# Graph network kernel, final update: node-row product made at the end of attention, means taken behind the message product, four node blocks per PSUM bank

## The reference, cut to what matters

```python
x = layernorm(x + attention_layer(x, edges))
h = relu(concat(x[src], x[dst]) @ Wm1 + bm1)
h = relu(h @ Wm2 + bm2)
messages = h @ Wm3 + bm3
agg = segment_sum(messages, dst) / clip(count, 1)
upd = relu(concat(x, agg) @ Wn1 + bn1) @ Wn2 + bn2
out = layernorm(x + (x + upd))
```

## Time and profile before

| | us |
|---|---|
| median of 3 runs | 1838.62 |
| lowest and highest | 1836.01, 1838.82 |
| the profiled execution, its own time | 1839.05 |
| its span in the trace | 1837.3 |
| PE busy | 1631.2 (89%) |
| DVE busy | 1577.7 (86%) |
| ACT busy | 1296.8 (71%) |
| POOL busy | 1176.0 (64%) |

### The profile page before, as it was taken

One profiled execution on the slowest core, in us unless ns is written; L12 is line 12 of the kernel. 1 busy time (PEld: TensorE's weight loads), 2 busy tenths in 40 slices (PEclk: granted clock), 3 DMA queues, 4 the chain that ended last, 5 costly groups with the idle time before them and its releaser, 6 DMA issues.

```text
span 1837.3 us, 52399 instructions
## 1 busy us (share of the span) xinstructions
PE 1631.2 (89%) x15380; PEld 1447.3 (79%) x15380; DVE 1577.7 (86%) x3374; ACT 1296.8 (71%) x2335; POOL 1176.0 (64%) x1197
## 2 busy tenths in 40 slices
PE   4778888777778777699999999999999999999986
PEld 3568777666667665499999999999999999999964
DVE  6999999778878767499999999999999999999976
ACT  5145777777777776577777777777777777777741
POOL 3135777767776612577777777777777777777710
PEclk9999999889898878799999999999999999999999
DMA  4135677788788734555555555555555555555511
GB/s 116 39 77 114 133 139 144 149 142 158 149 158 148 145 69 128 140 140 140 140 141 141 139 140 140 141 140 140 139 140 140 139 139 140 139 140 139 140 50 36
DMA packets 142000, 237.54 MB, mean 129 GB/s; under 512 B 27997, under 2 KB 92849, under 8 KB 141914
## 3 DMA queue, kind: packets, MB, share of 16 engines
q0 software_dynamic: 49632, 143.79, 32.4%
q1 hardware_dynamic: 89128, 91.13, 21.2%
q10 hardware_dynamic: 3154, 1.60, 0.4%
HBM read 186.67 MB, written 10.68 MB: 107 GB/s over the span
## 4 chain that ended last, share of the span: by engine, by line
PE 57%; DVE 1%; issue 0%; ACT 0%; DMA 0%; POOL 0%; POOLq 0%; DVEq 0%
PE ps L1300 12%; PE ps L1301 10%; PE ps L1306 10%; PE ps L1280 9%; PE psA L1318 6%; PE ps L1275 5%; PE ps L1285 2%; PE ps L1042 1%; PE ps L1053 1%; PE ps L1050 1%; PE psA L1061 0%; DVE x L1114 0%; DMA ga<-table_a,idx 0%; ACT u L1075 0%; POOL ga L1253 0%
## 5 line engine op out<-in xcount | busy, mean ns | idle before, releaser
L1253 POOL DMA_INDIRECT ga<-table_a,idx x784 | 766.8, 978 | 244.4 <-issue 82.6
L637 POOL DMA_INDIRECT head_n<-scr_eye,row_at x250 | 329.0, 1316 | 226.7 <-PE psC L683 106.2
L1300 PE MATMUL ps<-wm_hi,h_hi 128*128 128x256 f32 x1568 | 411.3, 295 | 0.7 <-ACT h_hi L1352 0.7
L1301 PE MATMUL ps<-wm_lo,h_hi 128*128 128x256 f32 x1568 | 390.8, 282 | 0.0
L1356 ACT ACTIVATE h<-ps 128x512 bf16<-128x512 f32 x392 | 234.1, 597 | 191.1 <-PE ps L1306 190.4
L1300 PEld LDWEIGHTS ps<-wm_hi,h_hi 128*128 128x128 f32 x1568 | 295.8, 189 | 31.8 <-ACT h_hi L1352 26.8
L1432 DVE TENSOR_TENSOR h<-rest,h 128x512 bf16<-128x512 f32 x392 | 269.4, 687 | 53.0 <-ACT h L1360 53.0
L1427 DVE SCALAR_TENSOR_TENSOR rest<-ps,h 128x512 f32<-128x512 f32 x392 | 268.6, 688 | 46.9 <-ACT h L1356 39.2
L1301 PEld LDWEIGHTS ps<-wm_lo,h_hi 128*128 128x128 f32 x1568 | 296.0, 189 | 0.0
L697 PE MATMUL psC<-ring_n,ring_m 128*126 x1320 | 229.2, 313 | 57.1 <-DVE ring_n L916 29.0
L1421 DVE SCALAR_TENSOR_TENSOR h_lo<-ps,h_hi 128x512 fp32r<-128x512 f32 x392 | 264.3, 692 | 3.1 <-ACT h_hi L1352 3.1
(11 more groups left out here) (192 smaller groups left out, 2529.0 us busy)
## 6 DMA issues: line engine op xcount, KB each, us to landing
dstb<-scr_dst SPq DMA_DIRECT2D x196, 126.0 KB
cnt<-stage SPq DMA_DIRECT2D x125, 195.3 KB
cnt<-stage SPq DMA_DIRECT2D x125, 109.9 KB
ga<-table_a,idx POOLq DMA_INDIRECT x784
bw<-table_b SPq DMA_DIRECT2D x196, 63.0 KB
table_b<-cnt SPq DMA_DIRECT2D x12, 336.0 KB
head_n<-scr_eye,row_at POOLq DMA_INDIRECT x250, 6.2
table_a<-pr SPq DMA_DIRECT2D x12, 224.0 KB
```

The lines of the kernel that those rows point to most:

```text
L637: pool.indirect_dma_start(head_n[:, w % HEADS, s, :], None, scr_eye, bass.IndirectOffsetOnAxis(ap=row_at[:, w % ROWS_AT, s:s + 1], axis=0) ...
L1253: pool.indirect_dma_start(ga[:, u, k, :], None, table_a, bass.IndirectOffsetOnAxis(ap=idx[:, u, k:k + 1], axis=0)).then_inc(gathered[u][k] ...
L1300: pe.matmul(ps2[q][:, t % 2, :], hi, w_hi[:, k, :], start=False, stop=True, skip_group_check=True)
L1301: pe.matmul(ps2[q][:, t % 2, :], hi, w_lo[:, k, :], start=False, stop=True, skip_group_check=True)
```

## The change

The product of `x1T` with `wa[0]` is taken out of Update and made at attention's end, into `T.xw` (2 x 3125 columns). `T.xw` is allocated for the whole program, and during attention serves as slots 0 and 1 of the probabilities; slots 2 and 3 are a tensor of their own, `upper`. So three of its products may be made once the last chunk of sums has been added (before the transposes of chunk 7), and eleven stand behind PE's last L741. They go through three PSUM banks; DVE copies ten of them out and ACT four.

In Update ACT writes each half of `T.xw` into the PSUM bank of `u1` ahead of the product with `msg`, which then accumulates on it. `T.agg` is no longer scaled; the scaling by `T.inv` is done on the product with `Wm3`, in the step that makes `msg`. The last product of a cut goes to one bank with four blocks side by side; ACT writes the bias `bb` there first, and DVE takes the cut in one instruction (`2 * x1 + bank`). Two small bf16 products with ones and a bias row open the two banks once. The load of `wn1` moves from SP's end of the sweep to attention's end, between `w` and `b1`, and PE waits for the three loads there (48 in place of 32).

The core of the diff:

```diff
+CUT_BLKS = 4
+NODE_CUTS = [(a * BLK, min(NBLK, a + CUT_BLKS) * BLK) for a in range(0, NBLK, CUT_BLKS)]
...
-        pr = sb("pr", [BLK, PR, N], fp32)
+        upper = sb("upper", [BLK, 2, N], fp32)
+        pr = [T.xw[0:BLK, 0, :], T.xw[0:BLK, 1, :], upper[:, 0, :], upper[:, 1, :]]
...
+        xw_banks = [psO[0], psO[1], psD]
+        XW = 2 * len(NODE_CUTS)
+        EARLY = 3
+        def xw_taken(n):
+            odd = [i for i in range(n + 1) if i >= XW // 2 and i % 2]
+            return (1, len(odd)) if n in odd else (0, n + 1 - len(odd))
...
             sp.dma_start(w.rearrange("p (c h) -> p c h", c=2), wm1.rearrange("(c f) h -> f c h", c=2)).then_inc(loaded, 16)
+            sp.dma_start(T.wa[:, :, :], wn1.rearrange("(c f) h -> f c h", c=2)).then_inc(loaded, 16)
...
-            pe.wait_ge(loaded, 32)
+            pe.wait_ge(loaded, 48)
+            def node_products(first, end):
+                for n in range(first, end):
+                    a, z = NODE_CUTS[n // 2]
+                    if n >= len(xw_banks):
+                        eng, count = xw_taken(n - len(xw_banks))
+                        pe.wait_ge(xw_read[eng], count)
+                    pe.matmul(xw_banks[n % len(xw_banks)][:, 0:z - a], T.wa[:, 0, (n % 2) * P:(n % 2 + 1) * P], T.x1T[:, a:z],
+                              start=True, stop=True).then_inc(xw_done, 1)
             for c in range(CH):
+                if c == CH - 2:
+                    pe.wait_ge(chunk_added, (2 * TURNS_A + 1) * CH + len(banks))
+                    pe.wait_ge(edges_read, DCUTS)
+                    node_products(0, EARLY)
...
+            node_products(EARLY, XW)
...
+            def copy_products(first, end):
+                for n in range(first, end):
+                    if xw_taken(n)[0] == 0:
+                        a, z = NODE_CUTS[n // 2]
+                        dve.wait_ge(xw_done, n + 1)
+                        dve.tensor_copy(T.xw[:, n % 2, a:z], xw_banks[n % len(xw_banks)][:, 0:z - a]).then_inc(xw_read[0], 1)
...
+                if c == CH - 1:
+                    copy_products(0, EARLY)
+            copy_products(EARLY, XW)
```

Update, PE:

```diff
+        for bank in self.banks:
+            pe.matmul(bank[:, :], T.ones_b[:, :], T.bias_b[:, :, :].rearrange("p t h -> p (t h)"), start=True, stop=True,
+                      skip_group_check=True).then_inc(self.u2_opened, 1)
...
-                pe.wait_ge(self.mean_ready, c + 1)
...
+                pe.wait_ge(self.msg_ready, c)
                 for m in range(2):
                     n = 2 * (c - 1) + m
-                    if n >= 4:
-                        pe.wait_ge(self.u1_ready, n - 3)
-                    pe.matmul(psU[n % 4][:, 0:z - a], T.wa[:, 0, m * P:(m + 1) * P], T.x1T[:, a:z], start=True, stop=False)
-                    if m == 0:
-                        pe.wait_ge(self.msg_ready, c)
-                    pe.matmul(psU[n % 4][:, 0:z - a], T.wa[:, 1, m * P:(m + 1) * P], msg[:, (c - 1) % 2, 0:z - a], start=False, stop=True).then_inc(self.u1_done, 1)
+                    pe.wait_ge(self.u1_seeded, n + 1)
+                    pe.matmul(psU[n % 4][:, 0:z - a], T.wa[:, 1, m * P:(m + 1) * P], msg[:, (c - 1) % 2, 0:z - a],
+                              start=False, stop=True, skip_group_check=True).then_inc(self.u1_done, 1)
...
-                for i, b in enumerate(range(a // BLK, z // BLK)):
-                    if b >= 2:
-                        pe.wait_ge(self.u2_read, b - 1)
+                pe.wait_ge(self.u2_seeded, c - 1)
+                for i in range((z - a) // BLK):
                     for k in range(2):
-                        last = pe.matmul(psV[b % 2][0:BLK, 0:D], u1[:, c % 2, k, i * BLK:(i + 1) * BLK], T.wb[:, k, :], start=(k == 0), stop=(k == 1))
-                    last.then_inc(self.u2_done, 1)
+                        last = pe.matmul(psV[c % 2][:, i, :], u1[:, c % 2, k, i * BLK:(i + 1) * BLK], T.wb[:, k, :],
+                                         start=False, stop=True, skip_group_check=True)
+                last.then_inc(self.u2_done, 1)
```

Update, ACT and DVE:

```diff
+        def seed_u1(c):
+            a, z = cuts[c]
+            for m in range(2):
+                act.activation(psU[(2 * c + m) % 4][:, 0:z - a], T.xw[:, m, a:z], ACT.Copy).then_inc(self.u1_seeded, 1)
+        for c in range(2):
+            seed_u1(c)
...
+                if c >= 2:
+                    act.wait_ge(self.u2_read, c - 1)
+                else:
+                    act.wait_ge(self.u2_opened, c + 1)
+                blks = (z - a) // BLK
+                act.activation(psV[c % 2][:, 0:blks, :], T.bb[0:BLK, :].rearrange("p (o f) -> p o f", o=1).broadcast_to([BLK, blks, D]),
+                               ACT.Copy).then_inc(self.u2_seeded, 1)
+                if c + 2 < CUTS:
+                    act.wait_ge(self.u1_ready, 2 * c + 2)
+                    seed_u1(c + 2)
...
-                for k in range(2):
-                    last = dve.tensor_tensor(T.agg[:, k, a:z], T.agg[:, k, a:z], T.inv[:, a:z], ALU.mult)
-                last.then_inc(self.mean_ready, 1)
...
-                dve.scalar_tensor_tensor(T.x1[:, bs, :], T.x1[:, bs, :], 2.0,
-                                         T.bb[0:BLK, :].rearrange("p (o f) -> p o f", o=1).broadcast_to([BLK, z // BLK - a // BLK, D]),
-                                         ALU.mult, ALU.add).then_inc(self.doubled, 1)
...
-                dve.scalar_tensor_tensor(self.msg[:, (c - 1) % 2, 0:z - a], self.has[:, (c - 1) % 2, 0:z - a], T.b3[:, 0:1], psM[(c - 1) % 2][:, 0:z - a],
-                                         ALU.mult, ALU.add).then_inc(self.msg_ready, 1)
+                step(dve.tensor_tensor(at, psM[(c - 1) % 2][:, 0:z - a], T.inv[:, a:z], ALU.mult))
+                dve.wait_ge(self.has_ready, c)
+                dve.scalar_tensor_tensor(at, self.has[:, (c - 1) % 2, 0:z - a], T.b3[:, 0:1], at, ALU.mult, ALU.add).then_inc(self.msg_ready, 1)
...
-                for b in range(a // BLK, z // BLK):
-                    dve.wait_ge(self.u2_done, b + 1)
-                    dve.tensor_tensor(T.x1[:, b, :], T.x1[:, b, :], psV[b % 2][0:BLK, 0:D], ALU.add).then_inc(self.u2_read, 1)
+                dve.scalar_tensor_tensor(T.x1[:, bs, :], T.x1[:, bs, :], 2.0, psV[(c - 3) % 2][:, 0:(z - a) // BLK, :], ALU.mult, ALU.add).then_inc(self.u2_read, 1)
```

More of the change, by code:

```diff
@@ L403, in _, with attention @@
             act.activation(T.hx[:, :, D:D + 1], onesf[0:BLK, 0:NBLK + 1].rearrange("p (b o) -> p b o", o=1), ACT.Copy)
-def attention(nc, T, scr_eye, wm1, bm1, table_a, table_b):
+def attention(nc, T, scr_eye, wm1, bm1, wn1, table_a, table_b):
     with ExitStack() as ctx:
@@ L668, in sum_chunk @@
                     for k in range(2):
-                        last = pe.matmul(bank[0:BLK, a * W2:(a + 1) * W2], pr[:, (first + k) % PR, b * BLK:(b + 1) * BLK],
+                        last = pe.matmul(bank[0:BLK, a * W2:(a + 1) * W2], pr[(first + k) % PR][:, b * BLK:(b + 1) * BLK],
                                          hx[:, bass.ds(t * BPT + first + k, 1), 0:W2].rearrange("p o w -> p (o w)"), start=(k == 0), stop=(k == 1))
@@ L849, in _ @@
                     act.activation(b_st[:, s, 0:i, 1, :], rest[:, s, 0:i, :], ACT.Copy).then_inc(part_ready[1], 1)
+            for n in range(XW):
+                if xw_taken(n)[0] == 1:
+                    a, z = NODE_CUTS[n // 2]
+                    act.wait_ge(xw_done, n + 1)
+                    act.activation(T.xw[:, n % 2, a:z], xw_banks[n % len(xw_banks)][:, 0:z - a], ACT.Copy).then_inc(xw_read[1], 1)
         @block.vector
@@ L999, in __init__ @@
         self.T, self.out = T, out
-        self.cuts = [(a * BLK, min(NBLK, a + self.CB) * BLK) for a in range(0, NBLK, self.CB)]
-        CW = self.CB * BLK
+        self.cuts = NODE_CUTS
+        CW = CUT_BLKS * BLK
         self.has = sb("has", [P, 2, CW], fp32)
@@ L1006, in __init__ @@
         self.psM = [bank[:, :, :].rearrange("p t h -> p (t h)") for bank in ps2]
-        self.psV = psA
-        self.mean_ready = sem("mean_ready")
+        self.banks = psA
+        self.u2_opened = sem("u2_opened")
+        self.psV = [bank[0:BLK, :].rearrange("p (b f) -> p b f", f=D) for bank in psA]
+        self.u1_seeded = sem("u1_seeded")
+        self.u2_seeded = sem("u2_seeded")
         self.has_ready = sem("has_ready")
@@ L1130, in vector, with messages @@
                 dve.tensor_scalar(T.den[:, bs], T.mv[:, bs, 1], EPS_LN, None, ALU.add).then_inc(self.var_ready, 1)
-def messages(nc, T, table_a, table_b, scr_dst, bm3, wm3, bn1, wn1, wn2, bn2, out):
+def messages(nc, T, table_a, table_b, scr_dst, bm3, wm3, bn1, wn2, bn2, out):
     with ExitStack() as ctx:
@@ L1539, in gnn_kernel @@
             index_tables(nc, src, dst, x, w0, att, wm2, bm2, T, scr_tile, scr_dst, scr_win, scr_pass, scr_eye, table_b)
-            attention(nc, T, scr_eye, wm1, bm1, table_a, table_b)
+            attention(nc, T, scr_eye, wm1, bm1, wn1, table_a, table_b)
         T.agg = sb("agg", [P, 2, NPAD], fp32)
@@ L1547, in gnn_kernel @@
```

(2 more changed lines are left out.)

43 lines of the change are left out of this document (22 added, 21 removed).

## The result

| | before | after |
|---|---|---|
| first measurement: median, lowest to highest (4 executions each) | 1838.46, 1836.01 to 1838.82 | 1813.26, 1810.59 to 1819.71 |
| ratio after/before, 95% interval | | 0.9862 [0.9837, 0.9887] |
| profiled execution, span | 1839.05, 1837.3 | 1810.60, 1808.8 |
| all measurements of this study, median, lowest to highest | 1838.35, 1824.75 to 1848.08 (58 executions) | 1819.58, 1810.59 to 1827.55 (24 executions) |

The change made the kernel faster, and by more than the range allowed: 1813.3 against 1819 to 1829. Three later measurements of the same kernel gave medians of 1819.4, 1821.3 and 1819.5, all inside the range. So two questions stand: whether the sums for the stages held, and where the other microseconds of the first measurement came from.

A forecast was written before the change was run, and what follows sets the result against it. Most of the chain lies in the unedited sweep; in Update PE and DVE are both loaded, each waiting once for the other. 1839.05 - 15.7 - 0.3 = 1823.05, median 0.43 lower: 1822.6 us, range 1819 to 1829.

The forecast's parts named there:

- Update, -15.7: Update stage: event-by-event sum with DVE the bound at 5.3 a cut; 15.7 us shorter, from 13.5 to 17.5.
- The period of 8.59 before: Update before: 8.59 us a cut, PE working 7.04 and standing 1.55 in L1061; DVE busy some 6.6.
- The start of Update, 0.5 earlier at low clock: Update's first cut: PE again starts at low clock, so L1042 of cut 0 ends at 1778.7, 0.5 earlier.
- Means behind the product: Update on DVE: loses L1091 (1.18 a cut), gains a multiplication from PSUM (0.73 plus 0.04).
- Attention's end, -2.2 and +1.9: Attention's end: tables 2.2 us earlier by PE's clock, stretch up to the sweep 1.9 longer; -0.3 taken in all.
- The sweep, nothing: The sweep: forecast had no change in its time.
- Low clock under the late products: Rival, attention's end: products run at low clock, sweep starts 8.3 later, 1831, or 1826 if only the last six; 0.16.
- ACT as the bound: Rival, Update: a PSUM write costs 1.1, not 0.6, giving 5.7 a cut; 1826 or 1829; chance 0.12.
- DVE as the real bound of the kernel before: Rival, Update: the change saves only its own DVE work, about 1.3 a cut, 8 in all; 1831; chance 0.05.
- Slower by placement: Rival, sweep: moved buffers make gathers or matmul operands cost more; 1852 at 0.15 us a group; chance 0.03.
- a larger gain than forecast: Rival: attention's end shorter by the full 2.2 and Update by 17.5; 1819; chance 0.02.
- How the numbers follow: Step setting 1822.6 and range 1819 to 1829 from the rivals; faster by over 0.2% 0.95, within 0.02, slower 0.03.

The follow-up runs named there:

- e6_one_block: Changed kernel with one block per bank again for the last product, doubling and bias back on DVE; 1832.57 us, one execution, Update 57.5.
- e3_move_alone: Kernel with only the moved product, keeping the old means and one block per bank; 1834.37 us, ratio 0.9979 to before, Update 59.7.
- e8_warm: Changed kernel plus bf16 products nobody reads, put on PE where it stands at the sweep's end; 1817.73 us, Update 43.1.
- e5_means_ahead: Changed kernel with the scaling of `T.agg` back ahead of the product with `Wm3`; 1827.55 us, one execution, Update 45.5.
- e1_layout: Kernel before with only the changed kernel's buffer allocation, all work as before; 1839.55 us, ratio 0.9999 to before.
- e2_no_move: Changed kernel with the `x1T` product back in Update and none at attention's end; 1828.27 us, ratio 0.9947 to before, Update 54.0.
- again: The changed kernel as it is, measured once more; 1819.42 us, ratio 0.9899 to before.
- after_again3: The changed kernel as it is, in the last of its repeat measurements; 1819.46 us, ratio 0.9907 to before.

## Why the prediction was right or wrong

- **Update, -15.7: right, small by 0.9.** The stand in L1061 went with the banks (`e6_one_block` brings it back), DVE and PE came out nearly equal (5.11 and 5.10), and the single wait for the root is there (1.80 against 2.1). The term that was off is DVE's sum per cut, 5.3: it is 5.11, since the statistics take 1.40 and not 1.52 up to the next instruction. PE has 5.10 a cut and not 5.36, since its last product is 1.74 and not 2.0. The last cuts, with no `msg` left to make, came at 3.9 and 3.7, forecast 4.2 and 3.9.
- **The period of 8.59 before: read in part.** The forecast took it for two loaded engines that each wait once for the other. DVE also stood 1.28 a cut for the root, behind PE's products and the relu, so the period was a round over PE, ACT and DVE. The forecast for Update didn't need this, as the shared banks break the round. The expectations for `e3_move_alone` and `e6_one_block` did, and their periods missed.
- **The start of Update, 0.5 earlier at low clock: right.** Its `msg` started 4.64 after the row that opens it (1767.01 against 1762.37), where the sum had 1778.7, the end of the product, against 1774.25: 4.45. I took the low clock as given; `e8_warm` shows it can be had back for some idle matmuls.
- **Means behind the product: costed within the sum, not apart.** `e5_means_ahead` shows no gain from this part.
- **Attention's end, -2.2 and +1.9: right.** 2.4 saved on the products of chunk 7, tail +1.8. The sum in between was loose: a last copy at 751 to 752, less 2.2, against 750.0, gives -1.2 to -0.2, where the text has -0.3 to +1.5. The copy from PSUM is 0.68, taken 0.65: the upper end of 0.41 to 0.73, to which the Trainium skill ("VectorE: DVE Perf Modes", section "Mode 2×_2P — use both read ports for one tensor") had pointed.
- **The sweep, nothing: right on average.** 1020.9 to 1026.2 in the four profiles of the changed kernel, 1024.1 before. `e1_layout` shows no effect of placement.
- **Rivals.** Low clock under the late products: no, the granted clock was 1.00 from 726 to 742, over a stand of 1.22 too. ACT as the bound: no, a write is 0.59, by starts 0.52. DVE as the real bound of the kernel before: no, it stood 1.28 a cut for the root, and with PE's work put back (`e2_no_move`) PE's own 6.78 set the pace. Slower by placement: no. The last, a larger gain than forecast (0.02, 1819), was the nearest to the first measurement, but not by its mechanism: Update's -16.6 is short of -17.5, and the copies lengthened the tail by 1.8, which that rival left out.
- **What failed is what the sum put at nothing.** The forecast had no term for attention's loop and the sweep, nor for the chunks of the tables ahead of chunk 7, and gave them no spread in the step "How the numbers follow". Between the first two profiles they moved by -5.6 (ahead of the mask product), -3.2 (the sweep) and -2.7 (the tables beyond the forecast 2.2). That makes 11.5 of the 12.5 by which the span fell further than 16.0; Update's 0.9 is most of the rest. The change is not shown to cause them: the same kernel, run again, had loops of 616.2 to 621.9 against 615.1 before. The range took in only the bounds of the unknown costs, and read three runs within 2.8 us of each other as the kernel's spread. 58 executions of before cover 1824.75 to 1848.08, with a standard deviation of 4.9. So a median of four can be off by some 5 either way (an estimate: twice 4.9 / 2), and such a range needs about that much more on each side. By all measurements the gain is 18.8 (1838.35 to 1819.58), and 15 to 19 in each of the three later ones, against the forecast 16.0; 1822.6 lies 3 above the median. That the first measurement came out 6 below the later ones was luck as far as is known; its cause is open.

## What to carry to other kernels

When an edit relieves one engine, look first at the hand-over that stands between it and the next: moving a product away gave 3 us while a bank was handed back block by block, and 8 once it was handed back a cut at a time. Then follow the whole round, over every engine in it: part of what the move saved was spent again on ACT, by writes that stood ahead of a root for which DVE, and behind it PE, was waiting. Where PE stands for a few microseconds ahead of fp32 products on the critical path, look at the granted clock behind the stand; useful work put there (or, failing that, idle matmuls) can be worth as much as an engine's work removed. And before taking three close runs for the spread of a kernel, look for stretches in its profile where the clock goes up and down: judge an edit by its own stretch, and leave room for the others in the range.

## What the runs showed of the hardware that was not expected

- Executions of one kernel on one chip differ by up to 23 us (31 executions of before, beside `again`, 1824.75 to 1848.08). Among the profiles attention's loop differs most (610 to 623).
- Stands of the same length do not always cost the clock: of two of 2.71 in `e3_move_alone`, a cut apart, one was followed by a product of 1.84, the other by one of 2.92. At the start of Update, behind stands of 2.71 and 1.93, the eight records of the same code took from 5.22 (`after_again3`) to 6.32 (the first profile of after), and 3.52 where PE had been kept at work (`e8_warm`).
- fp32 products accumulate on what ACT wrote into the bank, at no extra cost on PE (0.84 a matmul of 500 columns, as before), and ACT's writes follow each other every 0.52.
